# Part of three hidden-layer sums moved between the last turned tiles, and one key projection moved behind two score tiles, in a four-block graph network

## The reference, cut to what matters

```
y = cond_layer_norm(x, cond, s1, b1)
q, k, v = y@wq+bq, y@wk+bk, y@wv+bv            # 4 heads of 128
x = x + softmax over the edges(q k^T) v @ wo + bo
y = cond_layer_norm(x, cond, s2, b2)
x = x + relu(y @ m_w1 + m_b1) @ m_w2 + m_b2
```

## Time and profile before

| | us |
|---|---|
| median of three runs | 949.19 |
| the three runs | 948.27, 950.81, 949.19 |
| profiled execution, its own time | 949.91 |
| its span | 948.1 |

### The profile page before, as it was taken

The page is one execution under the profiler, slowest core; times in us unless marked ns, Lnnn a source line. Parts: engine busy times, 40 slices in busy tenths (PEclk is TensorE's granted clock), DMA queues, the critical chain, the costliest instruction groups (busy, mean ns, idle before and its releaser), DMA issues.

```text
span 948.1 us, 18288 instructions
## 1 busy us (share of the span) xinstructions
PE 851.4 (90%) x6760; PEld 747.0 (79%) x6760; DVE 658.6 (69%) x1305; ACT 456.7 (48%) x764; POOL 513.6 (54%) x601
## 2 busy tenths in 40 slices
PE   3899869999999899999989999989999989888786
PEld 2798857878998788989887989878898969765456
DVE  8999888792476676266667256577437677679896
ACT  5777563333565224466233456323346624245664
POOL 7677624257632466843177753256664229347771
PEclk9999978999999999999989999999999998978899
DMA  5100000133200123300015220003330002101121
GB/s 129 35 0 0 20 25 20 51 100 89 79 1 1 34 54 113 114 23 2 12 36 156 81 65 1 13 23 95 87 100 12 1 1 78 34 1 29 43 57 55
DMA packets 49362, 44.34 MB, mean 47 GB/s; under 512 B 6014, under 2 KB 37154, under 8 KB 49300
## 3 DMA queue, kind: packets, MB, share of 16 engines
q1 hardware_dynamic: 47492, 40.21, 14.8%
q10 hardware_dynamic: 1808, 3.31, 1.2%
HBM read 42.04 MB, written 1.33 MB: 46 GB/s over the span
## 4 chain that ended last, share of the span: by engine, by line
PE 61%; DVE 20%; issue 6%; ACT 5%; POOL 4%; DVEq 2%; DMA 1%; SPq 1%; POOLq 0%
PE psum L1644 19%; PE psum L1638 16%; PE psum L1740 10%; PE psum L1713 5%; PE psum L1662 5%; DVE arena L2099 2%; ACT arena L1487 2%; PE psum L1686 2%; DVE arena L929 1%; PE psum L851 1%; DVE stats L2227 1%; POOL ringw L1329 1%; DVE hot_dst L966 1%; DVEq L2331 1%; DVE hot_dst L2326 1%
## 5 line engine op out<-in xcount | busy, mean ns | idle before, releaser
L1270 POOL TENSOR_SCALAR acc<-acc,rden,flag 128x628 f32<-128x628 f32 x80 | 69.4, 868 | 111.3 <-DVE rden L2095 110.8
L1740 PE MATMUL psum<-ringw,arena 128*128 128x512 f32 (+1 forms) x480 | 119.2, 397 | 3.8 <-DVE arena L2107 2.5
L1644 PE MATMUL psum<-arena 128*128 128x384 f32 (+5 forms) x675 | 115.6, 324 | 0.0
L1638 PEld LDWEIGHTS psum<-arena,ringw 128*128 128x128 f32 x768 | 113.1, 190 | 0.4
L1638 PE MATMUL psum<-arena,ringw 128*128 128x314 f32 x768 | 113.3, 309 | 0.0
L1644 PEld LDWEIGHTS psum<-arena 128*128 128x128 f32 (+1 forms) x675 | 104.9, 189 | 6.9 <-DVE arena L2099 1.1
L1740 PEld LDWEIGHTS psum<-ringw,arena 128*128 128x128 f32 (+1 forms) x480 | 86.9, 186 | 25.0 <-DVE arena L2107 3.5
L1662 PE MATMUL psum<-ident,acc 128*128 128x128 f32 (+1 forms) x560 | 81.8, 278 | 18.5 <-DVE acc L2008 14.7
L1638 PE MATMUL psum<-arena 128*128 128x314 f32 (+1 forms) x480 | 88.1, 322 | 6.3 <-DVE arena L2099 5.6
L2079 DVE SCALAR_TENSOR_TENSOR arena<-psum,cols,arena 128x628 fp32r<-128x628 f32 x32 | 27.9, 872 | 88.1 <-ACT arena L1474 88.1
L1662 PEld LDWEIGHTS psum<-ident,acc 128*128 128x128 f32 (+1 forms) x560 | 66.7, 142 | 27.5 <-DVE acc L2008 17.5
(11 more groups left out here) (285 smaller groups left out, 1922.9 us busy)
## 6 DMA issues: line engine op xcount, KB each, us to landing
raw<-in_L_gnn_m_w SPq DMA_DIRECT2D x16, 256.0 KB
xn<-in_L_gnn_m_w SPq DMA_DIRECT2D x16, 256.0 KB
raw<-in_L_gnn_wv SPq DMA_DIRECT2D x8, 256.0 KB
xn<-in_L_gnn_wv SPq DMA_DIRECT2D x8, 256.0 KB
raw<-in_L_gnn_wq SPq DMA_DIRECT2D x8, 256.0 KB
xn<-in_L_gnn_wq SPq DMA_DIRECT2D x8, 256.0 KB
raw<-in_L_gnn_wk SPq DMA_DIRECT2D x8, 256.0 KB
xn<-in_L_gnn_wk SPq DMA_DIRECT2D x8, 256.0 KB
```

The costliest lines, as they stand in the source:

```text
L1270: g.tensor_scalar(pbuf[:, k % 4, 0:NW], pbuf[:, k % 4, 0:NW], rden[:, k:k + 1], flag[:, 1, k % NT:k % NT + 1], ALU.mult, ALU.mult).then_in ...
L1638: ins = pe.matmul(big[buf(u)][0:l.shape[1], h, 0:HW], l, r[:, h * HW:(h + 1) * HW], start=(i == 0), stop=(i == len(terms) - 1))
L1644: ins = pe.matmul(to, l, r, start=(i == 0), stop=(i == len(terms) - 1))
L1740: ins = pe.matmul(brow(ROWBLK[f"{name}{t}"])[0:KEYS[t], :], l, r, start=(pieces[0] + i == 0), stop=(pieces[-1] == KT - 1 and i == len(term ...
```

## The change

In the text below a window's row gives its bounds, its length, then busy time (and instructions) of PE, PE's weight loads, DVE, ACT and POOL, the granted clock, the DMA share and GB/s. The change has four parts, in each of the four blocks.

- The list `SECOND_NORM` takes the place of `norm_order(1)`: turned tile 2 is done ahead of conditions 3 and 4, and turned tiles 3 and 4 (`LATE`) leave the list. They are turned by `turn_late` into the `row` ring.
- On PE the hidden sums are cut in halves: the first half of `m0`, turned tile 3, the first half of `m1`, turned tile 4, the first half of `m2`, and then the second halves of `m0`, `m1`, `m2`, and both halves of `m3`. DVE takes row 4 and the rest of turned tile 2 before `centred` 3.
- The fourth head's keys, `k3`, are projected after the second score tile and not ahead of the first, on PE, ACT and DVE alike.
- The orders around these are refitted. ACT writes the high parts of two MLP weights at once after turned tile 2 and those of the condition weights after all four hidden tiles. POOL takes the rest of `W1` 1 among the first scores, the rest of `W1` 2 ahead of the last deviation, and three bias additions among the deviations. DVE does its four weight products for the last layer (L2139, L2144) between query and key tiles and no longer between hidden tiles.

```diff
+SECOND_NORM = ["c1_0", "c1_1", "t1_0", "c1_2", "t1_1", "t1_2", "c1_3", "c1_4"]
+LATE = ["t1_3", "t1_4"]
 ATT = attention_order(True)
+ATT.insert(2, ("k", HEADS - 1))
+ATT_ACT.insert(2, ("k", HEADS - 1))
+QK = [("q", h) for h in range(HEADS)] + [("k", h) for h in range(HEADS - 1)]
-BLOCK_ROW = ... [f"wo{t}" for t in range(NT)] + [f"m2_{t}" for t in range(NT)]
+BLOCK_ROW = ... [f"wo{t}" for t in range(NT)] + LATE + [f"m2_{t}" for t in range(NT)]
...
 # POOL
-                rests(WO + NT - 2, 0, KT + 4 - NT)
+                rests(WO + NT - 2, 0, KT + 3 - NT)
                 for k in range(HEADS * NT):
+                    if k == NT:
+                        rests(W1, 1, 2)
...
                 for t in range(NT):
+                    if t == NT - 1:
+                        rests(W1, 2, 3)
                     rstd_of(LN_BLK + it * 2 * NT + NT + t, t)
-                rests(W1, 2, KT)
-                for t in range(NT):
+                    if t < NT - 2:
+                        add_bias(1, t, 2)
+                rests(W1, 3, KT)
+                for t in range(NT - 2, NT):
                     add_bias(1, t, 2)
-                    if t in (1, 2):
-                        rests(W2, t - 1, t)
-                rests(W2, 2, KT)
+                rests(W2, 0, KT)
...
 # ACT
                     if t == 2:
                         act.wait_ge(row_full, ROWBLK["wo4"] + nr + 1)
-                    if t >= 2:
-                        highs((W1, W1, W2)[t - 2], (2, 3, 0)[t - 2], (3, 4, 1)[t - 2])
-                highs(W2, 1, 2)
+                        highs(W1, 2, KT)
+                highs(W2, 0, 2)
...
-                    for i in ((), (), (0,), (1, 2, 3))[o] if it < BLOCKS - 1 else ():
-                        high(S_BLK + PERBLK + i, condw[:, i, :], it)
+                for i in range(4) if it < BLOCKS - 1 else ():
+                    high(S_BLK + PERBLK + i, condw[:, i, :], it)
...
 # PE
+                    if n in ("c1_0", "c1_1", "c1_2", "t1_2"):
...
+                def turn_late(t):
+                    u = ROWBLK[f"t1_{t}"]
+                    free_row(pe, u, nr)
+                    pe.wait_ge(big_read, BIGBLK[f"c1_{t}"] + nb + 1)
+                    for k in range(KT):
+                        ins = pe.transpose(brow(u)[:, k * P:(k + 1) * P], ybuf[:, t % 2, k * P:(k + 1) * P], ident[:, :])
+                    ins.then_inc(row_full, 1)
+                def hidden_sums(o, h):
+                    u = BIGBLK[f"m{o}"]
+                    if h == 0:
+                        free_big(pe, u, nb)
+                        pe.wait_ge(split_done, S_BLK + W1 + o + 1 + ns)
+                        pe.wait_ge(big_read, BIGBLK["t1_2"] + nb + 1)
+                    elif o == 0:
+                        pe.wait_ge(row_read, ROWBLK["t1_4"] + nr + 1)
...
+                for o in range(KT - 1):
+                    hidden_sums(o, 0)
+                    if o < len(LATE):
+                        turn_late(NT - len(LATE) + o)
+                for o in range(KT - 1):
+                    hidden_sums(o, 1).then_inc(big_full, 1)
+                hidden_sums(KT - 1, 0)
+                hidden_sums(KT - 1, 1).then_inc(big_full, 1 + BIG_SPARE)
...
 # DVE
+                for what, h in QK:
+                    projected(what, h)
+                    if 1 <= QK.index((what, h)) <= 4:
+                        folded(QK.index((what, h)) - 1)
...
                 for t in range(NT):
-                    centred(1, t, it)
+                    if t < NT - 2:
+                        centred(1, t, it)
                     if t < NT - 1:
                         out_row(t + 1)
-                    else:
-                        turned_rest(1, t - 2, it)
+                    if t == NT - 2:
+                        turned_rest(1, t - 1, it)
+                    if t >= NT - 2:
+                        centred(1, t, it)
                     scaled(1, t, it)
...
+                hidden(0)
+                hidden(1)
+                hidden_rest(0)
+                hidden(2)
+                hidden_rest(1)
+                hidden_rest(2)
+                hidden(3)
+                hidden_rest(3)
```

More of the change, by code:

```diff
@@ L110 @@
 ROW_SPARE = -3 * NT % NROW
-BLOCK_ROW = [f"v{t}" for t in range(NT)] + [f"spare{i}" for i in range(ROW_SPARE)] + [f"wo{t}" for t in range(NT)] + [f"m2_{t}" for t in range(NT)]
+BLOCK_ROW = [f"v{t}" for t in range(NT)] + [f"spare{i}" for i in range(ROW_SPARE)] + [f"wo{t}" for t in range(NT)] + LATE + [f"m2_{t}" for t in range(NT)]
 L3_ROW = [f"H{d}{t}" for d in "bf" for t in range(NT)]
@@ L1469, in act_l2, with projected @@
                 next_bias(0)
-                for i, to in enumerate((qT, kT)):
-                    for h in range(HEADS):
-                        u = BIGBLK["qk"[i] + str(h)]
-                        act.wait_ge(big_full, u + nb + 1)
-                        act.activation(wide(to[:, 0, h, :]), bwide(u), ACT.Identity,
-                                       bias=bqk[:, i, bass.ds(it * KT + h, 1)]).then_inc(qkhi_up, 1)
-                        n = i * HEADS + h + 2
-                        highs((WK, WO, W1)[n // KT], n % KT, n % KT + 1)
+                def projected(what, h):
+                    i, to = {"q": (0, qT), "k": (1, kT)}[what]
+                    u = BIGBLK[f"{what}{h}"]
+                    act.wait_ge(big_full, u + nb + 1)
+                    act.activation(wide(to[:, 0, h, :]), bwide(u), ACT.Identity,
+                                   bias=bqk[:, i, bass.ds(it * KT + h, 1)]).then_inc(qkhi_up, 1)
+                    n = i * HEADS + h + 2
+                    highs((WK, WO, W1)[n // KT], n % KT, n % KT + 1)
+                for what, h in QK:
+                    projected(what, h)
                 for what, k in ATT_ACT:
-                    if what == "S":
+                    if what == "k":
+                        projected(what, k)
+                    elif what == "S":
                         act.wait_ge(big_read, BIGBLK[f"S{k}"] + nb + 1)
@@ L1727, in pe_l2, with projected @@
                     values(t)
-                for i in range(2):
-                    for h in range(HEADS):
-                        u = BIGBLK["qk"[i] + str(h)]
-                        free_big(pe, u, nb)
-                        q = (WQ, WK)[i] + h
-                        pe.wait_ge(split_done, S_BLK + q + 1 + ns)
-                        wide_mm(pe, u, sum([parts(wcol(RING_BLK + q, k), both(yT, k)) for k in range(KT)], [])).then_inc(big_full, 1)
+                def projected(what, h):
+                    u = BIGBLK[f"{what}{h}"]
+                    free_big(pe, u, nb)
+                    q = {"q": WQ, "k": WK}[what] + h
+                    pe.wait_ge(split_done, S_BLK + q + 1 + ns)
+                    wide_mm(pe, u, sum([parts(wcol(RING_BLK + q, k), both(yT, k)) for k in range(KT)], [])).then_inc(big_full, 1)
+                for what, h in QK:
+                    projected(what, h)
                 def row_terms(name, t, left, w, pieces):
@@ L1767, in pe_l2 @@
                         row_begin("wo", 1, qT, WO)
+                    if what == "k":
+                        projected(what, k)
+                        continue
                     u = BIGBLK[f"{what}{k}"]
@@ L1785, in pe_l2 @@
                 rows = 1
-                for n in norm_order(1):
-                    if rows < NT and n[0] == "c":
+                for n in SECOND_NORM:
+                    if n in ("c1_0", "c1_1", "c1_2", "t1_2"):
                         if rows > 1:
@@ new lines, in hidden, with hidden_rest @@
+                def hidden(o):
+                    u = BIGBLK[f"m{o}"]
+                    dve.wait_ge(big_full, u + nb + 1)
+                    if o >= 2:
+                        dve.wait_ge(hlo_up, it * KT + o - 1)
+                    dve.tensor_scalar(wide(rbuf[:, o % 2, :]), bwide(u), bqk[:, 2, bass.ds(it * KT + o, 1)], 0.0,
+                                      ALU.add, ALU.max).then_inc(big_read, 1 + BIG_SPARE * (o == KT - 1))
+                def hidden_rest(o):
+                    dve.wait_ge(hhi_up, it * KT + o + 1)
+                    dve.tensor_tensor(kT[:, 1, o, 0:NW], rbuf[:, o % 2, 0:NW], f32(kT[:, 0, o, 0:NW]), ALU.subtract).then_inc(hlo_up, 1)
```

81 lines of the change are left out of this document (35 added, 46 removed).

## The result

The changed kernel takes 927.97 us (median of 4 runs, 925.62 to 928.87), the kernel before 949.05 beside it (4 runs, 948.27 to 950.81): a ratio of 0.9772, with a 95% interval of 0.9749 to 0.9795, so 21 us less. The forecast was 929.3 us. The profiled execution took 925.62 us (span 923.8, mean granted clock 0.978), where the one of before took 949.91 (span 948.1, clock 0.958).

The account below looks back on a forecast made before the run. PE was taken as the bound, through its idle waits and low clock. Terms 15.0+5.9-2.0+0.4+0.6 = 19.9 us took the profiled 949.91 to 930.0, forecast as 929.3 because that profile lay 0.7 above the median; range 925 to 937.

Parts of the forecast that it names:

- The stall: Between condition 4 and the hidden sums: PE's wait on DVE's norm tail shrinks, 3.75 us per block, 15.0 us won.
- The clock: In the hidden stages: with 0.56 us idle left, granted clock stays at 1.00 throughout, 5.9 us won.
- Waits inside the hidden stage: Before the MLP rows: PE waits for DVE's rests of hidden tiles, -2.0 us, bounds 0 and -9.
- The keys: Around the first scores: about 0.1 us won, +0.6 us in all with the first block's table load.
- The first block's wait: First block, before the first MLP row ends: PE's wait of 0.42 us goes, +0.4 us.
- the next block: Condition and value weight loads fall 1.1 us behind; slack at the values some 0.3 to 0.6 us, cost 0.
- one of the signs by which the forecast was to fail: Hidden-stage clock below 1.00, weight-rest waits at value rows or conditions, or m0's second half waiting for turned tile 4.
- chain rival: Weight and condition loads on SP, ACT and POOL become the bound at the values: 934 or 941 us, chance 0.15.
- DVE's products: Weight products moved between query and key tiles, hidden there even at 1.90 us each: cost 0.
- clock rival: The clock falls all the same around the hidden sums, 5.9 us missing: 935.2 us, chance 0.10.
- the slower one: The low clock lasts through the MLP: in full about 1000 us, chance 0.04.
- The case in which that rule would have cost three losses per block: Hidden stage: three DVE rests each lose a whole GpSimd instruction of 1.29 us, ending 2.9 us behind m3, 11.7 in all.

Follow-up runs that it names:

- e9: Changed kernel with turned tiles 3 and 4 back ahead of all hidden sums on PE, other queues kept in their new order: 949.06 us, ratio 1.0.
- e3: Kernel before, with unused filler matmuls keeping PE busy in the gaps before turned tiles 3 and 4: 946.16 us, ratio 0.9971.
- e6: Changed kernel with tile 2 turned ahead of the end of PE's last output row, its rest on DVE ahead of that row's addition: 929.61 us, ratio 0.9778.
- e7: Changed kernel with the fourth head's keys one score tile later, behind the third: 925.98 us, ratio 0.9737.
- e1: Changed kernel with all four key tiles in front of the scores again: 930.02 us, ratio 0.9801.
- e8: e7 with the next block's first turned tile's rest ahead of the last MLP row's residual on DVE: 926.11 us, ratio 0.9735.
- e4: Changed kernel with DVE's four weight products back among the hidden tiles: 930.43 us, ratio 0.9798.
- e5: Changed kernel with POOL's second half of a block in its old order, PE, DVE and ACT unchanged: 949.44 us, ratio 0.9997.
- e10: Changed kernel with the fourth head's keys behind the fourth score tile on PE and DVE, behind the third on ACT: 926.87 us, ratio 0.977.

## Why the prediction was right

The forecast of 929.3 us lies 1.3 above the measured median, and its sum of 19.9 us stands against 20.0 measured in the blocks. The mechanism of the two large terms, stall and clock, is borne out by e9 and e3. That the total fits to 0.1 us is luck: the terms missed by -0.4, +0.1, +1.1, +0.4 and -1.1 us. Term by term:

- **The stall, 15.0 us: 14.6 measured.** The second stretch is 17.57 us shorter; the two late turned tiles, 0.74 per block, moved out of it into the next. The steps behind it came as worked out: 0.58 us idle (forecast 0.56), the turned tile steps 0.36 and 0.38 (0.36), `scaled` 4 started 3.13 us after the first half of m0 (2.98), and PE showed no wait at the second half of m0. e9 shows that it is the interleaving which removes the stall.
- **The clock, 5.9 us: 6.0.** It is 1.00 in all four hidden stages, so 62.28 less 4 x 14.08. e3 shows the same without any reordering. With the other queues left as they were, though, only 1.3 us of it reached the blocks' end there, so this term too leans on the refitted orders.
- **Waits inside the hidden stage, -2.0 us: -0.9.** 60.22 - 4 x 0.74 - 4 x 14.08. In the usual blocks the wait on PE's weight load is 0.19 us (forecast 0.25). The last block was mis-sized: 1.2 us forecast, and the wait is 0.38, the stage 0.20 us longer than the others. The mask tiles did keep ACT (767.29 to 770.99), and the high part of m0, whose relu had ended at 770.10, started at 770.89. But DVE's own order puts relu 1 (770.97 to 771.84) ahead of rest 0, so the delay fell into it, and rest 0 started 10.69 us after the first hidden matmul in this block (771.75 - 761.06) as in the second (478.39 - 467.70). The rests' durations in the second block:

```profile
478.10 1.29 POOL L1340 TENSOR_TENSOR ringw<-xn,ringw 128x512 fp32r<-128x512 f32 x1 [1.05 <-ACT ringw L1545]
478.39 1.67 DVE L2200 TENSOR_TENSOR arena<-acc,arena 128x628 fp32r<-128x628 f32 x1
...
480.95 1.69 DVE L2200 TENSOR_TENSOR arena<-acc,arena 128x628 fp32r<-128x628 f32 x2
482.70 1.46 PEld L1761 LDWEIGHTS psum<-ringw,arena 128*128 128x128 f32 x7 [0.19 <-DVE arena L2200]
```

  One rest took 1.67 us, beside POOL's instruction from 478.10 to 479.39, and the other two 1.69 together. The sum had 1.6, 1.1 and 0.8 for the three, 3.5 us; measured are 3.36. Over the kernel the 16 rests have a median of 0.90 us (0.80 to 1.83), below the 1.45 of the earlier trace rows.
- **The keys, +0.6 us: 1.0.** The argument was that the removed POOL wait is not won but handed on to DVE and ACT. The new wait of 0.51 us before the sixth score is the place. ACT's first turned score comes 33.59 us into the second block, where 33.69 was forecast (409.63 - 375.94) and 33.81 was the value before. The first stretch is 0.24, 0.22 and 0.17 us shorter in blocks 2 to 4, where about 0.1 was forecast, and 0.40 in the first, where the forecast had the exponential's table load besides.
- **The first block's wait, +0.4 us, and the next block at 0: together -0.67.** The wait of 0.42 did go. But the slack of 0.3 to 0.6 us that I left for the last value weight was not there, and in the first block PE waited:

```profile
355.72 0.96 PE L1731 MATMUL psum<-ringw,arena 128*128 128x512 f32 x3 [0.69 <-POOL ringw L1340]
```

  A wait for a weight's rest at the value rows was one of the signs by which the forecast was to fail, and in this place it did. It is the mildest form of the chain rival, 0.7 us in one place where I had priced 5 to 12 in three. It comes and goes between profiles, and what decides that was not found: e6 has it in the first block too (0.93 us), e7 and e1, whose last stretches are 99.62 and 99.67, do without it. In all three blocks a wait of 0.47 for the next block's first rest stands ahead of it, as before the change (0.48), and e8, which removes that wait, gets it back at POOL's weight: two limits almost level.
- **DVE's products, 0.** e4 prices their move at 4.9 us of PE's time in the changed kernel, most of it in the last block. The forecast did not need that number, since the products are out of the hidden stage; their new place cost nothing visible (the first stretch of e4 and the changed kernel agree within 0.2 us).

What the forecast did not say is how thin the cover is: POOL's new order was entered at a cost of 0, and e5 shows that without it 18.4 of the 20.0 us in the blocks are lost, by the medians all 21. The clock rival (935.2) and the slower one fell with the clock at 1.00.

The 1.3 us between forecast and median are not settled by a mechanism. They are smaller than the scatter outside the blocks; the profiled execution, for which the sum gives 930.0, took 925.62, and the 4.3 us between lie outside them.

## What to carry to other kernels

When PE stands for the last rows of its input, split its next sums by rows and start with the half whose rows are there; then price the queues behind it, for with the old order on POOL the stall merely moved behind the sums and the gain was nil (e5). An idle gap can have a second price in the clock: here 14.7 us of waiting had 6.0 us of slow matmuls behind it. Removing the slow matmuls alone brought 1.3 us in the blocks (e3). When an item is put into a hand-written order, try its neighbouring places as well, since one step later was worth another 2.7 us (e7) and two steps only 1.2 (e10).

## What the runs showed of the hardware

- **The same wait lowers the clock in one place and not in another.** In e5 PE stood once in each block, for 2.30 to 2.33 us, in an otherwise nearly fully busy stretch. After three of the four waits the granted clock fell (0.54 and 0.67 over the next 4.3 us in the second block), after that of the third block it stayed at 1.00; the levels are 1.2 and 2.4 GHz, and the 36 matmuls behind took 10.48 us against 8.87. A wait of 1.90 us in front of the first block's last value projections was followed by the low level in the kernel before (first row, 12 matmuls in 4.58 us) and by 1.00 in the changed one (second row, 3.00 us):

```profile
219.39 4.58 PE L1713 MATMUL psum<-ringw,arena 128*128 128x512 f32 x12 [1.90 <-DVE arena L2014]
...
218.89 3.00 PE L1731 MATMUL psum<-ringw,arena 128*128 128x512 f32 x12 [1.90 <-DVE arena L2056]
```

  So the length of one wait does not decide it, and what does was not tried. In the blocks, gaps of 0.45 (e3), 0.58 and 0.69 us, and those of up to 1.1 us before the change, left the clock at 1.00. Two gaps of 2.09 and 1.89 with only 0.63 us of turning between them (e9) lowered it in all four blocks, as 1.38 and 2.29 did before the change. The Trainium skill (TensorE: Matmul & The Clock Gate, "Part 1: The HAM clock gate") calls the low level the default state, which activity lifts; the traces agree in so far as the slow matmuls looked at here all follow a wait.
- **DVE and POOL delay each other, and who starts first loses nothing.** Of the changed kernel's rests of hidden tiles (128x628), the one of 1.67 us started 0.29 us after a POOL instruction (478.39 against 478.10), which itself took its usual 1.29. In the last block one started ahead of POOL's pair:

```profile
771.75 0.80 DVE L2200 TENSOR_TENSOR arena<-acc,arena 128x628 fp32r<-128x628 f32 x1
...
772.20 3.33 POOL L1340 TENSOR_TENSOR ringw<-xn,ringw 128x512 fp32r<-128x512 f32 x2 [1.78 <-ACT ringw L1545]
```

  It took 0.80, and POOL's pair 3.33 where such a pair takes 2.55 at 767.87; the pair's second instruction met DVE's next rest as well. The Trainium skill (SBUF — State Buffer, "SBUF: two separate sides") has the engine that starts first hold the shared port for its whole instruction; these rows agree. The case in which that rule would have cost three losses per block, 11.7 us in all, did not come, because in each block only one of the three rests was slow (1.67 in three blocks, 1.83 in the last). In e4's last block all three were, and POOL's six instructions there took 1.6 us each on average (3.12 for two, 6.57 for four).
- **The part of the kernel outside the blocks scatters by 8 us between profiles** of kernels that are the same there (369.3 to 377.1 us). Part of it is the clock: from the end of the wait of 1.90 us above to the first query matmul it is 4.42 us in the kernel before (223.81 - 219.39) and 2.84 in the changed one (221.73 - 218.89). What the rest hangs on was not tried.
